# A gated state-space and sparse-FFN block: silu taken by ACT itself, and the FFN tiles' normalisation and turn moved one step

## The reference

```
z = layernorm(x);  h = ctx;  xc = causal_conv4(in_proj @ h) + conv_b
u = silu(xc)                                   # 512 channels x 512 steps, each batch
dt, B, C = x_proj @ u;  delta = softplus(dt_proj @ dt + dt_b)
state[e, n] = state * exp(delta * A[e, n]) + (delta * u) * B[n]     # 16 states n, a scan over time
y = (sum_n state * C[n] + D * u) * silu(z)
x = x + tanh(g_xattn) * y
x = x + tanh(g_ffn) * FFN(layernorm(x))        # top-2 router over 32 experts of rank 16
```

## Time and profile before

| | |
|---|---|
| median of 3 runs | 546.57 us |
| the profiled execution | 550.42 us, of it a span of 548.6 us |
| PE busy | 490.2 us (89%) |
| DVE busy | 481.8 us (88%) |
| POOL busy | 456.5 us (83%) |
| ACT busy | 393.8 us (72%) |
| chain of work that ended last | PE 53%, DVE 21%, ACT 13%, issue 9%, POOL 2%, DMA 1% |
| table loads on ACT | before Ln (L938) 20, before the decays' Exp (L985) 20, each 1283 ns; one at the start |

### The profile page before, as it was taken

One profiled execution on the slowest core, in us unless ns is written; L12 is line 12 of the kernel. 1 busy time (PEld: TensorE's weight loads), 2 busy tenths in 40 slices (PEclk: granted clock), 3 DMA queues, 4 the chain that ended last, 5 costly groups with the idle time before them and its releaser, 6 DMA issues.

```text
span 548.6 us, 9113 instructions
## 1 busy us (share of the span) xinstructions
PE 490.2 (89%) x2962; PEld 361.4 (66%) x2962; DVE 481.8 (88%) x884; ACT 393.8 (72%) x704; POOL 456.5 (83%) x337
## 2 busy tenths in 40 slices
PE   6687989898888799999998999998999999899688
PEld 2156979767766486766776776657666666675654
DVE  3868999978989999979999999889899889999852
ACT  3268697847685878586886868595988888888542
POOL 0169999969999998979999999979799899887910
PEclk9656999999989899999999999999999999999799
DMA  5794000107520000047230000068100000000001
GB/s 102 265 340 158 1 2 1 39 7 268 193 76 2 2 1 32 27 154 254 78 97 1 20 2 20 1 192 289 63 1 21 19 22 10 11 20 20 1 21 38
DMA packets 18705, 39.37 MB, mean 72 GB/s; under 512 B 5585, under 2 KB 6353, under 8 KB 18658
## 3 DMA queue, kind: packets, MB, share of 16 engines
q1 hardware_dynamic: 18658, 38.79, 20.9%
HBM read 34.33 MB, written 4.46 MB: 71 GB/s over the span
## 4 chain that ended last, share of the span: by engine, by line
PE 53%; DVE 21%; ACT 13%; issue 9%; POOL 2%; DMA 1%; DVEq 0%; ACTq 0%; SPq 0%; POOLq 0%
PE p_s L744 12%; PE p_y L766 11%; DVE state L1228 10%; PE p_v L799 7%; PE p_f L790 6%; PE p_tr L711 3%; PE p_pr L667 3%; PE p_pr L674 3%; ACT da L985 2%; PE p_pr L686 2%; DVE x L1170 2%; DVE p_s L1228 2%; PE p_f L779 1%; ACT L938 1%; ACT p_s L985 1%
## 5 line engine op out<-in xcount | busy, mean ns | idle before, releaser
L564 POOL TENSOR_TENSOR state<-state,c_bc 128x1024 f32<-128x1024 f32 (+1 forms) x131 | 256.5, 1970 | 21.7 <-DVE state L1228 19.6
L744 PEld LDWEIGHTS p_s<-pair_b,du_t 128*128 128x128 f32 x1072 | 139.4, 198 | 41.9 <-issue 29.7
L744 PE MATMUL p_s<-pair_b,du_t 128*128 128x128 f32 x1072 | 152.8, 285 | 13.6 <-DVE state L1228 10.6
L549 POOL TENSOR_TENSOR dbu<-du,pair_b 128x1024 f32<-128x1024 f32 (+1 forms) x80 | 145.2, 1818 | 5.6 <-DMA pair_b<-bc_rows 4.2
L766 PE MATMUL p_y<-ident,state 128*128 128x128 f32 x1024 | 148.7, 275 | 0.0
L985 ACT ACTIVATE p_s<-delta,a_neg 128x512 f32<-128x512 f32 (+1 forms) x162 | 93.6, 581 | 66.9 <-DVE state L1246 33.5
L1228 DVE TENSOR_TENSOR_SCAN state<-da,p_s 128x512 f32<-128x512 f32 (+1 forms) x116 | 134.5, 1173 | 7.3 <-PE p_s L744 6.7
L766 PEld LDWEIGHTS p_y<-ident,state 128*128 128x128 f32 x1024 | 120.8, 143 | 23.7 <-issue 22.7
L985 ACT ACTIVATE da<-delta,a_neg 128x512 f32<-128x512 f32 (+1 forms) x158 | 100.4, 648 | 15.6 <-DVE state L1228 15.3
L1228 DVE TENSOR_TENSOR_SCAN state<-p_s,dbu 128x512 f32<-128x512 f32 (+1 forms) x100 | 98.3, 998 | 1.9 <-POOL dbu L549 1.8
L790 PE MATMUL p_f<-u_sb,h_t 128*128 128x512 f32 x112 | 56.9, 612 | 1.2 <-DVE gw L1329 1.2
(11 more groups left out here) (180 smaller groups left out, 662.5 us busy)
## 6 DMA issues: line engine op xcount, KB each, us to landing
c_bc<-bc_rows SPq DMA_DIRECT2D x32, 512.0 KB, 5.4
pair_b<-bc_rows SPq DMA_DIRECT2D x16, 512.0 KB, 6.2
xs<-in_x SPq DMA_DIRECT2D x16, 256.0 KB, 4.7
out<-ot SPq DMA_DIRECT2D x14, 256.0 KB, 2.0
cx<-in_ctx_t SPq DMA_DIRECT2D x4, 512.0 KB, 3.5
u_sb<-in_u_w SPq DMA_DIRECT2D x1, 1024.0 KB, 7.3
v_sb<-in_v_w SPq DMA_DIRECT2D x1, 1024.0 KB, 14.7
w_in<-in_in_w_t SPq DMA_DIRECT2D x1, 384.0 KB, 4.7
```

Source lines behind the costliest of these rows:

```text
L549: eng.tensor_tensor(dbu[:, i % 2, :, 0:w], du[:, 0:w].unsqueeze(1).to_broadcast([P, 2, w]), rows_of_b(p)[:, :, c0:c0 + w], ALU.mult).then_ ...
L564: eng.tensor_tensor(pair, pair, c_bc[:, 2 * p:2 * p + 2, c0:c0 + w], ALU.mult).then_inc(po_cs, 1)
L744: mm = eng.matmul(p_s[g % BANKS][:, t * P:(t + 1) * P], du_t[:, f % 2, t, :], diagonals_of(n // 2)[:, n % 2, c0 // P + t, :], start=(t == ...
```

## The change

ACT's table of functions has Silu, and two pairs of steps are replaced by it:

- `u`: ACT writes silu(v) straight to `u` from the convolved block (new `silu_u` on ACT), at the place where it wrote the tanh. DVE's product is gone, and so is the halving of the conv weights.
- z in phases 0 to 11: one ACT step `silu_z` at step 15, between `copy_du` and `silu_u`, takes the place of `z_part` 0 and 1 (steps 13 and 14) and of DVE's product (step 14). The factor tanh(g) moves into the scale of `copy_sz`. Phases 12 to 19 keep their two ACT parts and DVE's product.
- FFN tiles: `normed` stands at step 0, `turn_h` at step 1 and `copy_h` at step 2 for every T.
- POOL makes two more constants at the start and one operation fewer for each batch. The semaphore counts follow.
- The first function of the program, which brings the first table, is Silu, no longer Exp.

The diff, without its unchanged lines:

```diff
+        one = sb("one", [P, Q])
+        minus_one = sb("minus_one", [P, Q])
...
-        zr = sb("zr", [P, 2, 4, Q])
+        zr = sb("zr", [P, 2, 2, Q])
...
-        ac_th = sem("act_tanh_v")
+        ac_u = sem("act_u")
...
-        ve_u = sem("dve_u")
...
         def broadcasts_of_b(b, p):
...
-        ZOPS = 6
+        ZOPS = 5
...
+            eng.memset(one[:, :], 1.0).then_inc(po_k, 1)
+            eng.memset(minus_one[:, :], -1.0).then_inc(po_k, 1)
+            eng.wait_ge(po_k, 11)
...
             def scale_of_z(b):
...
-                    eng.wait_ge(ac_z, 2 * Q * (b - 1))
+                    eng.wait_ge(ac_z, Q * (b - 1))
...
-                eng.tensor_tensor(zr[:, b % 2, 0, :], zv[:, 1, :], half[:, :], ALU.mult).then_inc(po_zs, 1)
-                eng.tensor_tensor(zv[:, 0, :], zv[:, 1, :], minus_half[:, :], ALU.mult).then_inc(po_zs, 1)
+
+                plus, minus = (one, minus_one) if b + 1 < B else (half, minus_half)
+                eng.tensor_tensor(zr[:, b % 2, 0, :], zv[:, 1, :], plus[:, :], ALU.mult).then_inc(po_zs, 1)
+                eng.tensor_tensor(zv[:, 0, :], zv[:, 1, :], minus[:, :], ALU.mult).then_inc(po_zs, 1)
...
-                eng.wait_ge(po_zs, ZOPS * b + 5)
-                eng.wait_ge(ac_k, 2)
-                eng.tensor_scalar(zr[:, b % 2, 2:4, :], zr[:, b % 2, 0:2, :], gx[:, :], None, ALU.mult).then_inc(po_zs, 1)
...
             def small_projection(b, blocks):
...
-                    eng.wait_ge(ve_u, Q * b + Q if b else k + 1)
+                    eng.wait_ge(ac_u, Q * b + Q if b else k + 1)
...
-                    eng.wait_ge(ve_u, min(f + Q, BLOCKS))
+                    eng.wait_ge(ve_tap, 3 * min(f + Q, BLOCKS))
...
             def turn_sz(f):
-                eng.wait_ge(ve_sz, f + 1)
+                if f < SPLIT:
+                    eng.wait_ge(ac_z, f + 1)
+                else:
+                    eng.wait_ge(ve_sz, f - SPLIT + 1)
...
             def turn_h(T):
...
-                            eng.wait_ge(ve_k, 3)
+                            eng.wait_ge(ve_k, 1)
...
-                    if n == 1 and mid >= 0 and mid % Q == 0:
+                    if n == 1 and mid >= 0:
...
-                    if n == 15 and Q <= f < EARLY + Q and f % Q:
-                        turn_h(f - Q)
...
-            def tanh_v(q):
+            def silu_u(q):
...
-                eng.activation(conv_bank(q)[:, :], conv_v(q), ACT.Tanh).then_inc(ac_th, 1)
+                if q >= U_RING:
+                    eng.wait_ge(ac_skip, q - U_RING + 1)
+                    eng.wait_ge(ve_dl, q - U_RING + 1)
+                eng.activation(u[:, q % U_RING, :], conv_v(q), ACT.Silu).then_inc(ac_u, 1)
...
             def copy_small(b):
...
-                        eng.wait_ge(ve_u, min(f + Q, BLOCKS))
+                        eng.wait_ge(ac_u, min(f + Q, BLOCKS))
...
-            def copy_turn(kind, i, dest):
+            def copy_turn(kind, i, dest, scale=1.0):
...
-                eng.activation(dest, bank[:, :, 0:NS] if kind == "b" else bank[:, 0:blocks, :], ACT.Copy).then_inc(ac_turn, 1)
+                eng.activation(dest, bank[:, :, 0:NS] if kind == "b" else bank[:, 0:blocks, :], ACT.Copy,
+                               scale=scale).then_inc(ac_turn, 1)
...
+            def silu_z(f):
+                b, k, c0, w = PHASE[f]
+                eng.wait_ge(po_zs, ZOPS * (b + 1))
+                eng.wait_ge(s_x[b % 2][k], 16 * (b // 2 + 1))
+                if f:
+                    eng.wait_ge(pe_turn, TURN["sz", f - 1] + 1)
+                eng.activation(zh[:, 0:w], xs[:, b % 2, k, c0:c0 + w], ACT.Silu, bias=zr[:, b % 2, 1, k:k + 1],
+                               scale=zr[:, b % 2, 0, k:k + 1]).then_inc(ac_z, 1)
+
             def z_part(f, part):
...
-                    eng.activation(zh[:, 0:w], source, ACT.Identity, bias=zr[:, b % 2, 3, k:k + 1],
-                                   scale=zr[:, b % 2, 2, k:k + 1]).then_inc(ac_z, 1)
+                    eng.activation(zh[:, 0:w], source, ACT.Identity, bias=zr[:, b % 2, 1, k:k + 1],
+                                   scale=zr[:, b % 2, 0, k:k + 1]).then_inc(ac_z, 1)
...
             def copy_sz(f):
...
-                copy_turn("sz", f, sz_t[:, 0:PHASE[f][3] // P, :])
+                eng.wait_ge(ac_k, 2)
+                copy_turn("sz", f, sz_t[:, 0:PHASE[f][3] // P, :], gx[:, :])
...
             def place_residual(T):
...
-                    eng.wait_ge(ve_sz, T + 6 if T + 7 < F else F)
+                    f = T + 6 if T + 7 < F else F
+                    if f > SPLIT:
+                        eng.wait_ge(ve_sz, f - SPLIT)
...
-            eng.activation(table[:, :], minus_half[:, 0:1], ACT.Exp)
-            eng.wait_ge(ve_k, 2)
+            eng.activation(table[:, :], minus_half[:, 0:1], ACT.Silu)
+            eng.wait_ge(s_conv, 32)
...
-                tanh_v(q - 1)
-            tanh_v(Q - 1)
+                silu_u(q - 1)
+            silu_u(Q - 1)
...
-            eng.wait_ge(ve_k, 4)
+            eng.wait_ge(ve_k, 2)
...
-                        tanh_v(4)
+                        silu_u(4)
...
-                    if n == 0 and mid >= 0 and mid % Q == 0:
+                    if n == 0 and mid >= 0:
...
-                    if n == (1 if mid % Q else 2) and mid >= 0:
+                    if n == 2 and mid >= 0:
...
-                    if n == 13:
+                    if n == 13 and f >= SPLIT:
...
-                    if n == 14:
+                    if n == 14 and f >= SPLIT:
...
+                        if f < SPLIT:
+                            silu_z(f)
...
-                            tanh_v(f + 5)
-                        if Q <= f < EARLY + Q and f % Q:
-                            normed(f - Q)
+                            silu_u(f + 5)
...
-            def silu_u(q):
-                eng.wait_ge(ac_th, q + 1)
-                if q >= U_RING:
-                    eng.wait_ge(ac_skip, q - U_RING + 1)
-                eng.scalar_tensor_tensor(out=u[:, q % U_RING, :], in0=conv_bank(q)[:, :], scalar=1.0, in1=conv_v(q),
-                                         op0=ALU.add, op1=ALU.mult).then_inc(ve_u, 1)
-
...
             def silu_z(f):
...
-                eng.wait_ge(ac_z, 2 * f + 2)
+                eng.wait_ge(ac_z, SPLIT + 2 * (f - SPLIT) + 2)
...
-            eng.tensor_scalar(cw[:, :, :], cw[:, :, :], 0.5, None, ALU.mult).then_inc(ve_k, 1)
-            eng.tensor_scalar(cb[:, :], cb[:, :], 0.5, None, ALU.mult).then_inc(ve_k, 1)
-            eng.wait_ge(ve_k, 2)
...
             def taps(q):
...
-            taps(0)
-            for q in range(1, Q):
+            for q in range(Q):
...
-                silu_u(q - 1)
-            silu_u(Q - 1)
...
-                    if f == 0 and n == 6:
-                        silu_u(4)
...
-                        eng.wait_ge(ve_k, 5)
+                        eng.wait_ge(ve_k, 3)
...
-                        eng.wait_ge(ve_k, 6)
+                        eng.wait_ge(ve_k, 4)
...
-                        silu_z(f)
+                        if f >= SPLIT:
+                            silu_z(f)
...
-                    if n == 15 and f + 5 < BLOCKS:
-                        silu_u(f + 5)
...
```

## The result

The changed kernel takes 569.2 us (median of 4 runs, 566.3 to 574.4) against 546.5: ratio 1.0385, interval 1.0341 to 1.0428. Slower, as forecast, but by 3.9% where 1.4% was forecast, and outside the range. The profiled execution took 570.91 us, its span 568.9 us, 20.3 us longer than before.

What follows compares the result with a forecast made beforehand. DVE was taken to set the pace early, with PE and DVE both full later. Start, phase 0 and phase ends summed to +7.8 us: 558.2 on the profiled 550.42, 554.4 against the median 546.57; range 550 to 559, wider 544 to 565.

Steps and rivals of the forecast that it cites:

- The loads: ACT: 27 new table loads, 12 pairs at phase ends, 35 us of ACT time, 68 loads in all.
- rival 4: ACT: each load between unlike functions holds it for twice its length; +33, about 588 us; chance 0.03.
- Early ends: Phase 2's end, worked out: DVE waits 2.2 us for ACT's first decay, +1.0; phase 0 +0.2, phase 4 -0.7.
- The start and phase 0: Before the loop -1.9 us; phase 0 +2.1 for block 4's Silu between two loads, +0.2 at its end.
- Late ends, the direct part: Phase 9's end, worked out: PE waits 2.6 us at `turn_h` in step 1 for ACT's tile; +2.3.
- Turning phases: Ends of phases 2, 6 and 10, before turning phases 3, 7 and 11: 0, -0.5 and -0.5 us.
- The moved tile: FFN tile moved from step 15, half-width phases 12 to 18: zero, bounds -3 and +3 us.
- So PE falls 2.3 us back, having saved the 1.09 already.: Phase 9's end: PE's delay at `turn_sz` behind `copy_h`, counted in full because PE is full; +2.3 us.
- Phase 5's end as "an early one", and 11's at +1.2: Phase 5's end: +1.0, as an early one by its slack; phase 11's: +1.2, no u, half the products.
- Rival 1: PE's waits are absorbed and only DVE's side counts, late ends costing like early ones: +4.0, 550.6 us; chance 0.22.
- Rival 2: Silu needs no load beside Exp, loads stay near 41, DVE never waits: about -13 us, 533.6; chance 0.14.
- Rival 3: The PE and ACT loop sets every phase from 5 on, half-width phases lose too: +16, 562.6 us; chance 0.19.

Runs made afterwards that it cites:

- e1: The changed kernel with Tanh in place of every Silu, so no table is switched for them: 540.28 us, ratio 0.9816 to the kernel before.
- e4: The kernel before with only the FFN tiles moved to steps 0, 1 and 2 for every T: 549.07 us, ratio 0.9997.
- e3: The changed kernel with nine unused identity matmuls before PE's tile wait in phases 6, 8, 9, 10 and 12: 559.85 us, ratio 1.0183 to the kernel before.
- e8: The kernel before with z alone by one Silu at step 15 in phases 0 to 11, behind the copy of du: 571.51 us, ratio 1.0403.
- e7: The kernel before with z alone by one Silu at step 13 in phases 0 to 11: 546.65 us, ratio 0.9951.
- e5: The kernel before plus one unused 128x1 Silu at step 15 of phases 0 to 11, adding 24 loads: 561.39 us, ratio 1.0219.
- e2: The changed kernel with the FFN tile normalised at step 15 before the two Silus (T not a multiple of 4): 574.1 us, ratio 1.0450 to the kernel before.

## Why the prediction was right in sign and wrong in size

- **The loads: right.** 68, a pair at each of the 12 phase ends, 1.28 us each and the next activation 0.02 us behind (108.25 to 109.55). e1 puts all 27 at 29.5 us with everything that they brought about, less than their 35 us of length. The activation before a load is followed by no gap either (108.23 to 108.25), so rival 4 falls. The Trainium skill ("ScalarE: Activation LUTs", What ACT_TABLE_LOAD costs) adds a drain of 1380 ns to a switch; no gap in this trace shows it, so the measurement decides against it here.
- **Early ends: right.** Worked out: DVE waits 2.2 us, +1.0. Measured: 1.99 us, +1.1, in phases 1 and 2. Phase 3's end is alike: 2.02 us before phase 4's first scan. Phase 3 shows -0.1 in the table because PE's turning work took up phase 2's +1.1 by its fourth scan, as forecast. Phase 4's end was to win 0.7 and won 0.6. Phase 5's +0.1 holds a piece of luck: in that trace the kernel before had 3.4 us of half clock there, and the changed kernel, at full clock, gained 1.1 us on it by the tenth scan.
- **The start and phase 0: two errors and chance.** -2.5 and +1.6 us, where I had -1.9 and, with the phase's end, +2.3. Over all traces the start is worth 1.3 us. In phase 0 I counted both loads around block 4's Silu. The first (35.59 to 36.87) fell into ACT's wait for the taps, of which 2.19 us were left before the Silu, and cost nothing. The phase's end cost +0.9 between its last scan and the next first one, not +0.2.
- **Late ends, the direct part: right.** Worked out: PE waits 2.6 us for the tile and falls 2.3 us back. Measured: 2.46 and 0.71 us at the end of phase 9, and 2.3 us in each of phases 9 and 10. Phase 8's end, put at +1.0, cost as much.
- **Turning phases: about right.** -0.8 and -0.3 us for 7 and 11, -0.5 each forecast.
- **The moved tile: right** by itself (e4), zero.
- **The step that failed: "So PE falls 2.3 us back, having saved the 1.09 already."** The sum priced PE's wait by its length and by nothing else. The clock stands in no term of it. The change put up to 3.4 us of waiting, in one or two pieces, in front of an engine that was 96% busy. At half clock for 6.8, 6.8 and 10.2 us, PE did 11.9 us less than it would have, and e3 gives back 10.7 of the 20.3 us. The trace before had full clock in phases 6 to 12, but it also had the warning, in phase 5, where PE waited 2.08 us before 180.89 and 1.25 us before 183.27:

```profile
178.00:182.00 4.00, 1.92 (x16) 1.54 (x14) 3.96 (x12) 3.79 (x8) 3.90 (x4) 1.00 0.01 2
182.00:186.00 4.00, 2.75 (x5) 1.19 (x5) 3.93 (x8) 3.96 (x6) 4.00 (x3) 0.60 0.00 0
```

- **The rest of the sum: nearer than its parts.** The 9.6 us that e3 leaves stand against my 7.8. Phases 5 to 12 lost 8.9 us there, where I had 6.1 for the ends 5 to 11; the start and phase 0 gave 1.5, where I had a loss of 0.4. The two errors partly cancel, and that is luck.
- **Phase 5's end as "an early one", and 11's at +1.2:** both brought a fall of the clock, in phases 6 and 12. With the clock whole (e3) phases 6 and 12 still lost 2.3 and 1.5 us. So the half-width stretch was not free of the loads either: its first phase had PE's longest wait, 3.44 us in the matmul's row and 3.7 by the weight load, from the last pair of loads.
- **Rival 1** fell with the 2.3 us of phases 9 and 10.
- **Rival 2** fell with the 68 loads, and e1 shows what it would have been worth: without loads the change would win 1.8%, not 2.4%. I had set its likelihood low for the right reason.
- **Rival 3** had the right place (PE, copy, loads, tile, turn) and, at +16, came nearest, for a cause that it did not name. Its 5.4 us do not follow from its own condition. At +2.3 for all seven ends from 5 to 11 it would add 10.0, without the two turning ones 4.9.

Of the signs named before, the loads, DVE's two idle times (1.99 and 2.02 us), block 3's u (19.19 us) and the turning phases came out. PE's wait for the tile in phases 8 to 11 was 2.02, 1.91, 2.46 and 0.60 us, so at phase 11 it was not there.

What stays open: why the clock stays whole in phases 9 and 10 after waits of 1.91 and 2.46 us, each with one of 0.7 behind it, and falls in phase 6 after 2.14 and 0.71. No run separates that. It may be chance of position in time, which is not shown. This kernel's four runs spread from 566.3 to 574.4 us, where all runs of the kernel before stay within 546.0 to 551.8, and in the four the longer time goes with the lower mean clock (0.957 at 566.3, 0.954 at 567.5, 0.949 at 570.9, 0.940 at 574.4). How much of e8's 22 us is clock was not measured either.

## What to carry to other kernels

An engine with idle time has room for more work only where its idle time stands; ahead of a hand-over, its room is the lead that its buffers allow. A load pair with its Silu, at the step where the lead is full, cost less than the product that it saved (e7, 0.5% faster); two steps later it cost 4% (e8). And when TensorE is nearly full, price a new wait twice: once by its length, and once by half speed for some microseconds behind it; a few idle matmuls in the wait (e3) show which of the two it is. The trace before is the place to look first: if its clock has already fallen behind waits of that size, it can fall behind new ones.

## What the runs showed of the hardware

A load of ACT's table takes 1283 ns for Silu's as for Exp's and Ln's; a Silu takes what the Tanh or Identity in its place took (814 ns against 803 for z with scale and bias from memory, 615 against 596 for u). Tanh behind a Silu needed no load, nor did Identity behind the two (e5, e8). TensorE's granted clock fell to 1.2 GHz behind waits of 2.9 to 3.5 us in all in phases 6, 8 and 12 of the changed kernel and phase 8 of e2, and stayed there for 6.8 to 13.7 us, although PE had no gap of 0.1 us once the wait was over. In phases 9 and 10 it stayed at 2.4 GHz behind 2.6 and 3.2 us. With 2.17 us of matmuls of the identity in the wait (e3) it stayed at 2.4 GHz in all of these phases.
